# Two cross attention layers on one core: exponentials kept in the score bank, products of n and u1 made earlier, and a row term carried through DRAM

## The reference

```python
# x (32, 256, 512); ctx (32, 256, 256); all float32
q = x @ Wq + bq;  k = ctx @ Wk + bk;  v = ctx @ Wv + bv          # layer 0
w = softmax(q @ k.T / sqrt(512), axis=1)      # over the 256 query rows
y = w @ v + x
n = (y - mean(y)) * rsqrt(var(y) + 1e-6)
x = n * gamma + beta
Q = x @ Wq1 + bq1;  K = ctx @ Wk1 + bk1;  V = ctx @ Wv1 + bv1    # layer 1
a = softmax(Q @ K.T / sqrt(512), axis=-1)
out = x + (a @ V) @ Wo1 + bo1
```

## Time and profile before

| | us |
|---|---|
| median of 3 runs (lowest, highest) | 729.48 (728.43, 730.53) |
| the profiled execution, device time | 729.61 |
| its span, first to last instruction | 727.5 |
| mean granted TensorE clock, share of full speed | 0.993 |

### The profile page before, as it was taken

How to read it: one execution, slowest core, us unless ns; L and a number is a source line. 1 busy time by engine, 2 the same in 40 slices (tenths; PEclk the granted TensorE clock), 3 DMA queues, 4 the chain that set the end, 5 groups by cost and what they waited for, 6 DMA issues and landing times.

```text
span 727.5 us, 12504 instructions
## 1 busy us (share of the span) xinstructions
PE 691.4 (95%) x4107; PEld 598.8 (82%) x4107; DVE 571.3 (79%) x1235; ACT 429.7 (59%) x1040; POOL 495.7 (68%) x391
## 2 busy tenths in 40 slices
PE   8987999999999999999999999999999999999987
PEld 6864888888888888888888888888888888888876
DVE  4899587877968787787878778787877779787764
ACT  2745557466565756656575665757565575656542
POOL 0276958769495876949586794958678494957680
PEclk9999999999999999999999999999999999999999
DMA  8801004040120404012040402104040210401003
GB/s 296 282 1 57 32 1 145 1 145 0 47 97 0 144 0 144 0 61 83 0 144 0 144 0 84 61 0 144 0 144 0 90 55 0 144 0 59 1 0 117
DMA packets 30336, 49.50 MB, mean 68 GB/s; under 512 B 2160, under 2 KB 10352, under 8 KB 30320
## 3 DMA queue, kind: packets, MB, share of 16 engines
q1 hardware_dynamic: 30320, 49.29, 20.0%
HBM read 32.51 MB, written 16.78 MB: 68 GB/s over the span
## 4 chain that ended last, share of the span: by engine, by line
PE 51%; POOL 25%; issue 8%; ACT 8%; DVE 6%; DMA 1%; SPq 0%; POOLq 0%; DVEq 0%; ACTq 0%
PE bank L388 46%; POOL xprod L1177 10%; POOL r L1200 8%; PE bank L395 4%; POOL prod L1168 4%; ACT xT_hi L635 3%; POOL y_lo L1183 2%; ACT prod L721 2%; DVE n L835 1%; PE bank L408 1%; DVE n L1001 1%; ACT cn_even_hi L751 1%; ACT cT_even_hi L635 1%; ACT cn_odd_hi L751 1%; DMA wk_sb<-in_L_xattn_Wk_dram 1%
## 5 line engine op out<-in xcount | busy, mean ns | idle before, releaser
L1160 POOL TENSOR_TENSOR rstd<-var_eps,minus_half 128x2 f32<-128x2 f32 x32 | 22.4, 699 | 115.5 <-DVE var_eps L997 115.5
L633 ACT ACTIVATE y_hi<-bank,terms 128x512 fp32r<-128x512 f32 x64 | 44.1, 689 | 77.5 <-PE bank L388 77.2
L809 DVE SCALAR_TENSOR_TENSOR y_lo<-bank,terms,y_hi 128x512 fp32r<-128x512 f32 x64 | 45.6, 745 | 55.0 <-ACT y_hi L633 55.0
L1168 POOL TENSOR_TENSOR prod<-n,u_b 128x512 f32<-128x512 f32 x64 | 84.2, 1340 | 0.1
L1207 POOL TENSOR_TENSOR r<-r,beta_b 128x512 f32<-128x512 f32 x60 | 76.1, 1288 | 0.0
L1200 POOL TENSOR_TENSOR r<-n,gamma_b 128x512 f32<-128x512 f32 x60 | 75.7, 1307 | 0.0
L388 PE MATMUL bank<-xT_hi,wqk_hi 128*128 128x512 f32 x128 | 52.7, 412 | 14.9 <-DVE xT_lo L811 14.9
L965 DVE SCALAR_TENSOR_TENSOR w_lo<-e,rinv,w_hi 128x256 fp32r<-128x256 f32 x64 | 58.8, 976 | 4.1 <-ACT w_hi L700 4.1
L635 ACT ACTIVATE pc_hi<-bank 128x512 fp32r<-128x512 f32 x32 | 19.1, 598 | 68.4 <-PE bank L388 68.4
L635 ACT ACTIVATE xT_hi<-bank 128x512 fp32r<-128x512 f32 x64 | 33.0, 605 | 37.1 <-PE bank L395 37.1
L974 DVE SCALAR_TENSOR_TENSOR r<-bank,rinv,r 128x512 f32<-128x512 f32 x60 | 44.6, 745 | 12.7 <-PE bank L388 12.7
(11 more groups left out here) (197 smaller groups left out, 2413.5 us busy)
## 6 DMA issues: line engine op xcount, KB each, us to landing
out_dram<-r SPq DMA_DIRECT2D x15, 1024.0 KB, 5.0
x_even<-in_x_dram SPq DMA_DIRECT2D x8, 1024.0 KB, 7.4
ctxn<-in_ctx_dram SPq DMA_DIRECT2D x16, 512.0 KB, 5.5
x_odd<-in_x_dram SPq DMA_DIRECT2D x8, 1024.0 KB, 7.3
wq_sb<-in_L_xattn_Wq_dram SPq DMA_DIRECT2D x4, 256.0 KB, 3.2
wk_sb<-in_L_xattn_Wk_dram SPq DMA_DIRECT2D x2, 512.0 KB, 7.6
wv_sb<-in_L_xattn_Wv_dram SPq DMA_DIRECT2D x2, 512.0 KB, 9.6
wq_sb<-in_L_xattn_Wq_dram SPq DMA_DIRECT2D x1, 1024.0 KB, 11.4
```

Source lines behind the costliest of these rows:

```text
L633: i = act.activation(dst, at((name, k))[:], ACT.Identity, bias=bias)
L809: i = dve.scalar_tensor_tensor(dst, src, bias, high.bitcast(F32), ALU.add, ALU.subtract)
L1160: pool.tensor_tensor(rstd[:, q], var_eps[:, q], minus_half[:, q], ALU.pow).then_inc(rstd_ready, 1)
L1168: pool.tensor_tensor(prod[j % 2][:], N[:, j, :], u_b[1][:], ALU.mult).then_inc(prod_ready, 1)
```

## The change

Three edits.

1. Row term of layer 0: bank `rb`, its four TensorE transposes and ScalarE's copy are gone. SyncE writes `r0s` to a DRAM row of 512 values (`write_r0`, one element per descriptor), waits for it, and loads that row to all 128 partitions of RB (`spread_r0` on SyncE). The load waits also until the bias rows were added (`x_biased`). Both stand behind the context load and ahead of the store of the pair before. VectorE's `maxima0` waits for `rb_loaded`. In iteration 0 one such pair of transfers stands behind the first load of the next x, and a second one, for the next pair, behind the context load.
2. Exponentials: ScalarE reads E0 and writes the exponentials to the score bank (`probs0`), `w_hi` and `w_lo` read them there, and the bank is free only after `w_lo`. `neg0_ready` and the release of the bank come once per half.
3. Products of n and u1: blocks 0 and 1 are made in the same iteration, ahead of the second `rstd`, and both wait for both blocks of n; blocks 2 and 3 come first in the next iteration and wait for both as well. In the iteration before the last (`before_last`) both `rstd` come first. ScalarE sums blocks 0 and 1 at the very end of its iteration, 2 and 3 in the next one between the context's rounding and `y_hi`, that is ahead of `nT_hi`. `add_beta` is done for four blocks together, ahead of `add_bias`. In iteration 0 `next_row_terms0` moves ahead of `prepare1c`.

```diff
-FRONT = {"xT", "cT", "rb", "y", "s0", "rs", "wc", "pr"}
+FRONT = {"xT", "cT", "y", "s0", "rs", "wc", "pr"}
...
+    r0_rows = nc.dram_tensor("r0_rows", (J * P,), F32).ap()
...
+        def probs0(b, mt):
+            return at(("s0", b))[:, mt * T:(mt + 1) * T]
...
+            def write_r0(ready, spread_before):
+                sp.wait_ge(r0s_ready, ready)
+                if spread_before is not None:
+                    sp.wait_ge(rb_loaded, spread_before)
+                with nc.allow_non_contiguous_dma("512 row terms, one element each"):
+                    sp.dma_start(r0_rows.rearrange("(j p) -> p j", p=P), r0s[:]).then_inc(r0_written, 16)
+            def spread_r0(written, biased):
+                sp.wait_ge(r0_written, written)
+                if biased is not None:
+                    sp.wait_ge(x_biased, biased)
+                sp.dma_start(RB[:], r0_rows.partition_broadcast(P)).then_inc(rb_loaded, 16)
...
+                    if not it.back:
+                        write_r0(1, None)
+                        spread_r0(16, None)
                     sp.wait_ge(filled[BANK["cT", KC - 1]], cT_filled)
                     sp.wait_ge(cn_lo, cn_cut)
                     sp.dma_start(ctxn[:], rows_of(ctx_rows, upcoming)).then_inc(ctx_loaded, 16)
+                    write_r0(r0_made, r0_spread)
+                    spread_r0(r0_in_rows, rb_free)
...
-                    spread_r0(it)                      # TensorE
...
                 for b in range(2):                     # ScalarE, softmax0
-                    act.wait_ge(neg0_ready, it.times(2, b + 1))
                     for mt in range(RM):
                         q = b * RM + mt
-                        if mt == RM - 1:
-                            wait_emptied(act, it, "s0", b)
-                        e = act.activation(E0[:, b, mt, :], E0[:, b, mt, :], ACT.Exp, scale=-1.0,
+                        if mt == 0:
+                            act.wait_ge(neg0_ready, it.times(2, b + 1))
+                        e = act.activation(probs0(b, mt), E0[:, b, mt, :], ACT.Exp, scale=-1.0,
...
                 if it.back:                            # ScalarE, iteration
-                    row_terms(it, (0, 1))
+                    row_terms(it, (2, 3), 1)
+                    shifted_row_terms(it)
...
-                if it.front:
-                    copy_bank(it, "rb", 0, RB[:])
-                if it.back:
-                    row_terms(it, (2, 3))
-                    shifted_row_terms(it)
...
-                if it.more:
+                if it.more and it.back:
                     next_row_terms0(it)
+                if it.front:
+                    row_terms(it, (0, 1), 0)
...
                     if b == 0:                         # VectorE, maxima0
-                        wait_emptied(dve, it, "rb")
+                        dve.wait_ge(rb_loaded, it.times(16, 16))
...
-                        dve.scalar_tensor_tensor(W[1][:, b, mt, :], E0[:, b, mt, :], rinv0[:, q:q + 1],
-                                                 W[0][:, b, mt, :].bitcast(F32), ALU.mult, ALU.subtract)\
-                           .then_inc(w_lo, 1)
+                        i = dve.scalar_tensor_tensor(W[1][:, b, mt, :], probs0(b, mt), rinv0[:, q:q + 1],
+                                                     W[0][:, b, mt, :].bitcast(F32), ALU.mult, ALU.subtract)
+                    i.then_inc(emptied[BANK["s0", b]], 1)
...
+            def row_products(it, blocks, back):        # GpSimd
                 for j in blocks:
-                    pool.wait_ge(n_ready, it.times(J, j + 1 - J))
+                    pool.wait_ge(n_ready, it.times(J, max(j, blocks[-1]) + 1 - back * J))
...
                 if it.back:                            # GpSimd, iteration
-                    row_products(it, (0, 1))
+                    row_products(it, (2, 3), 1)
...
                 if it.back:
-                    add_beta(it, (0, 1))
+                    add_beta(it, range(J))
...
                 if it.front:
                     add_bias(it)
-                if it.back:
-                    add_beta(it, (2, 3))
-                if it.front:
-                    rstds(it)
+                    rstd_of(it, 0)
+                    if it.before_last:
+                        rstd_of(it, 1)
+                    if it.j is None and it.known == 0:
+                        wait_emptied(pool, it, "u1")
+                    row_products(it, (0, 1), 0)
+                    if not it.before_last:
+                        rstd_of(it, 1)
```

More of the change, by code:

```diff
@@ L36 @@
 EPS = 1e-6
[L39 removed]
+FRONT = {"xT", "cT", "y", "s0", "rs", "wc", "pr"}
 def tiles(name, n):
     return [(name, k) for k in range(n)]
[L46 removed]
+STEADY = (tiles("xT", 4) + tiles("cT", 2) + tiles("y", 2) + tiles("nT", 4) + tiles("s0", 2)
           + tiles("y1", 2) + [("wc", 0), ("rs", 0), ("wc", 1)] + tiles("s1", 2) + tiles("pr", 2) + tiles("pt", 2)
@@ L61, in place_banks @@
     for t in STEADY:
-        if t[0] in ("rb", "rs"):
-            bank[t] = (turn + (3 if t[0] == "rb" else 4)) % BANKS
+        if t[0] == "rs":
+            bank[t] = (turn + 4) % BANKS
         else:
@@ L258, in two_cross_attentions @@
         hi = {n: sem(f"{n}_hi_ready") for n in ("xT", "cT", "cn", "y", "w", "wc", "nT", "y1", "pt", "pc")}
-        cn_lo, w_lo, w_lo_added = sem("cn_lo_ready"), sem("w_lo_ready"), sem("w_lo_added")
+        cn_lo, w_lo_added = sem("cn_lo_ready"), sem("w_lo_added")
+        r0_written, rb_loaded = sem("r0_rows_written"), sem("rb_loaded")
         r0_ready, r0s_ready, exp0_ready = sem("r0_ready"), sem("r0s_ready"), sem("exp0_ready")
@@ L546, in weigh0 @@
             def weigh0(it, b):
-                pe.wait_ge(w_lo, it.times(2 * RM, (b + 1) * RM))
+                wait_emptied(pe, it, "s0", b)
                 if b == 0:
@@ L715, in bias_of_rows, with row_terms @@
                 act.activation(bias[j], bv0_b[:], ACT.Copy, scale=rs[:, j:j + 1]).then_inc(bias_ready, 1)
-            def row_terms(it, blocks):
+            def row_terms(it, blocks, back):
                 for j in blocks:
-                    act.wait_ge(prod_ready, it.times(J, j + 1 - J))
+                    act.wait_ge(prod_ready, it.times(J, j + 1 - back * J))
                     act.activation(prod[j % 2][:], prod[j % 2][:], ACT.Copy,
@@ L786, in iteration @@
                 if begin_it:
+                    next_row_terms0(it)
                     prepare1c(it)
@@ L940, in maxima0 @@
                                                      neg0[:, q:q + 1])
-                        i.then_inc(*((emptied[BANK["s0", b]], 1) if mt == RM - 1 else (neg0_ready, 1)))
+                    i.then_inc(neg0_ready, 1)
             def maxima1(it):
@@ L1154, in bv_wo, with rstd_of @@
                                        ALU.add).then_inc(bvwo_ready, 1)
[L1156 to L1162, removed]
+            def rstd_of(it, b):
+                pool.wait_ge(var_ready, it.times(2, b + 1))
+                q = slice(b * RT, (b + 1) * RT)
+                pool.tensor_tensor(rstd[:, q], var_eps[:, q], minus_half[:, q], ALU.pow).then_inc(rstd_ready, 1)
+            def row_products(it, blocks, back):
                 for j in blocks:
-                    pool.wait_ge(n_ready, it.times(J, j + 1 - J))
+                    pool.wait_ge(n_ready, it.times(J, max(j, blocks[-1]) + 1 - back * J))
                     if j >= 2:
-                        pool.wait_ge(r1_ready, it.times(J, j - 1 - J))
+                        pool.wait_ge(r1_ready, it.times(J, j - 1 - back * J))
                     pool.tensor_tensor(prod[j % 2][:], N[:, j, :], u_b[1][:], ALU.mult).then_inc(prod_ready, 1)
@@ L1180, in add_w_lo @@
             def add_w_lo(it):
-                pool.wait_ge(w_lo, it.times(2 * RM, 2 * RM))
+                wait_emptied(pool, it, "s0", 1)
                 pool.tensor_tensor(w_lo_sum.rearrange("p (b t) -> p b t", b=2), W[1][:, :, 0, :].bitcast(F32),
```

14 lines of the change are left out of this document (7 added, 7 removed).

## The result

The changed kernel takes 809.68 us (808.3 to 811.7, 4 runs), before 730.0: ratio 1.1096, 95% interval 1.1062 to 1.113. It is 11% slower; 708 was forecast, with 0.05 on the rival that a slow element write makes it slower. The profiled execution took 811.7, its span is 809.9, 82.4 us over the span before.

A forecast was written before the change was run, and what follows sets the result against it. TensorE, at 95%, was taken as the bound. 24.6 us of steady gains less 1.8 for prologue and 1.8 for tail gave 21.0 off 729.61: 708.6, said as 708, range 703 to 717.

The forecast's parts named there:

- The two transfers, steady: Element write, broadcast and store on SyncE in a steady iteration: claimed to cost nothing, with the write's landing free up to 4.0 us.
- D: Landing time of the element write of r0s to DRAM: taken as 3 us, bounds 2.0 and 9.8.
- the rival on the other side: Element write lands after more than 5.7 us, each us over 4.0 coming back 14 times; at 9.8, 790 us; chance 0.05.
- the prologue: Before iteration 1: RB lands at 38 (36.5 to 41), delaying maxima0; iteration 1 comes 1.8 us later (0.5 to 5).
- Wait for xT_lo: TensorE's wait each steady iteration: no product runs beside n, VectorE wins 1.77 us ahead of xT_lo; gain 0.85 us.
- Wait at row_sums: TensorE's wait for y_lo each iteration: w_lo falls from 4.05 to 1.68 us, y_lo comes before TensorE; gain 0.49 us.
- The rb transposes: Ahead of scores0 on TensorE: removing them lets the scores take their place, as y_lo ends just before; gain 0.39 us.
- Steady sum: Gains of the steady iteration together: 1.73 us a period, period 40.35, 24.6 us in all.
- Tail: Last iteration: sums ahead of nT_hi make y1 wait for its lo; costs 1.8 us (0 to 4).
- add_beta ahead of add_bias: Four add_beta behind y_lo on GpSimd delay the first bias: claimed hidden, with 1.4 us to spare.

The follow-up runs named there:

- e2_dram_alone: Kernel before with only the pair of DRAM transfers in place of the rb transposes; 819.54 us, ratio 1.1233.
- e4: Changed kernel with the DRAM row laid out by partition, 128 runs of 16 bytes, and RB read with a step of four; 708.53 us.
- e10: Changed kernel with, from the second write on, 512 single elements 512 bytes apart to another DRAM tensor, RB loaded from the first write's row; 711.59 us.
- e11: Changed kernel with the row written as 256 runs of 8 bytes and RB read with a step of two; 710.88 us.
- e13: e10 with 8 bytes instead of 512 from one single element to the next; 711.47 us.
- e9: Changed kernel writing, from the second write on, only one of four columns of r0s, 128 single 4-byte elements side by side; 809.23 us.
- e12_filler: Changed kernel with 22 useless matmuls put into TensorE's wait ahead of row_sums in iterations 1 to 14; 800.56 us.
- e1_no_dram: Changed kernel with the DRAM transfers undone, rb transposes and ScalarE's copy back; exponentials in the bank and moved products stay; 704.85 us.
- e6_bank_alone: Kernel before with only the exponentials put in the score bank; 717.24 us, ratio 0.9853.
- e5_no_dram_tail: e1_no_dram with ScalarE rounding nT ahead of the sums of products 2 and 3 in the last iteration; 700.73 us.

## Why the prediction was wrong

**The step that failed: "The two transfers, steady".** D was bounded by 2.0 and 9.8 and taken as 3, "nearer to the first", because the queue is empty. It is 8.2 (e2_dram_alone; SyncE's wait in the kernel after is 8.1). An empty queue was no reason for a short landing: behind the same queue the forms of e4 and e10 land after 1.4 and 1.8. The form of the write decides, which no term of the sum had. Of the two rows that I weighed, one was a store in large pieces, the other a load, and neither wrote single neighbouring elements: the value between them was a guess, and 0.05 for everything above 5.7 was far too little. The mechanism is the rival on the other side: a landing over 4.0 comes back in 14 iterations. The point from which it decides fits the runs as far as they go: landings of 3.2 and 3.9 us cost next to nothing (mean periods of 40.36 and 40.34 in e11 and e13), 1.4 wins no more (40.31 in e4), and 7.4 and 8.2 cost some 7 us a period. Nothing between 3.9 and 7.4 was run, and that each us comes back whole isn't shown: from 8.2 to 7.4 (e9) the mean period fell by 0.45, not 0.8.

**Its price was too small.** For 8.2 that rival gives 14 x 4.2 - 21 = 38 us slower, measured are 80. Of the missing 42: the store lands after 7.5 us, not 6.0 (14 x 1.5 = 21). It starts late: in the kernel after nothing moves for 2.7 us behind the broadcast's issue at 457.55, while in e13, with the same transfers in the same order up to the load of x, the first bytes show 0.9 us behind it (issue 477.49) and the store lands after 5.6. The context, issued earlier than in e13, comes only at 460.02 and can't be the cause of that; why the queue starts late behind the dense write stays open. Further, the clock, which I held at 0.993, falls in the waits (9, e12_filler); the prologue costs 6.0 instead of 1.8 (4), as the write holds RB until 42.4, beyond my 41. Some 8 us stay unassigned.

**The page.** "DMA: Bandwidth & Descriptors" of the Trainium skill has about 2 us fixed ("Anatomy of one DMA — SWDGE (gpsimd) path", a fit for transfers issued by GpSimd, which the prediction took over for SyncE's) and a read-modify-write under 512 B ("Specifications"). The trace doesn't agree with the first for this write, 8.2 us, and is not far off it for e4 and e10, 1.4 and 1.8. Being under 512 B isn't what is slow by itself: e10's elements have 4 bytes each. Read-modify-writes of one stretch one behind the other would fit the table above; the runs show the dependence on density, not that mechanism.

**Wait for xT_lo, 0.85:** right in kind, 1.1 in size. The row of the bracket counts from the modelled end of the last transpose. From the start of the x transposes to the first y matmul it is 239.16 - 235.52 = 3.64 us before and 2.54 in e1_no_dram (428.15 to 430.69).

**Wait at row_sums, 0.49:** right in kind, too small for the same reason. From the last matmul ahead of `row_sums` to its matmul with the sum of `w_lo` it is 1.35 us before (256.81 to 258.16) and 0.58 in e1_no_dram (408.13 to 408.71): 0.77. e6_bank_alone, which removes this wait alone, has a period shorter by 0.76. Its cause, `w_lo` at 4.05, was right too; that the moved products would remove half of it without the bank was not seen.

**The rb transposes, 0.39:** wrong, the period fell by 0.06. The step was that TensorE could take up the scores in the transposes' place, as `y_lo` ends 0.07 us before them. But the first score matmul starts 0.46 us after the end of `y_lo` before, 0.47 in e1_no_dram, and 0.45 in e4, without the transposes: `y_lo` set its start all along, and they lay in that lag. The row's order of two ends was no proof of which one TensorE waited for.

**Steady sum:** 1.73 forecast; e1_no_dram's period is 1.81 shorter, e4's 1.87. The errors of these three cancel.

**Tail, 1.8:** 1.7 in the kernel after, but 3.2 in e1_no_dram (632.02 to 702.3, before 660.40 to 727.5), where the wait is 3.0 us and the matmuls behind it are slower; e5_no_dram_tail takes it away. **add_beta ahead of add_bias:** hidden, as said.

## What to carry to other kernels

Small values that go through DRAM should be written as runs of 16 bytes or more, or apart from each other: 512 neighbouring 4-byte writes held the queue for 8 us here, the same 2 KB as 128 runs 1.4, and a reader can take the changed order with a step. With a step of four values VectorE's `maxima0` took 0.61 us a time instead of 0.42 (e4), with a step of two 0.42 (e11). Before such a write is put on a queue, ask what is issued behind it and by when that has to land; here a store that a scaling on GpSimd waited for closed the loop. Even a write that lands fast wants a look at the prologue, where nothing covers it. And where two bounds of an unknown are on both sides of the point that decides, the chance must lie on both sides too.

## What the hardware showed that I had not expected

The landing of the 2 KB write by its form: 8.2 us dense (7.4 with a quarter of the elements), 3.9 and 3.2 at half that density, 1.4 as 128 runs of 16 bytes, 1.8 as 512 elements far apart. The dense write's packets show for about 1 us, and for the rest of its 8 us the DMA engines show nothing. A store that is queued behind it before it has landed begins to move, stands still and goes on when the write ends: 10.5 us for a 1 MB store that took 5.0. And what is issued behind the landing still starts 2.7 us after its issue instead of 0.9 (the kernel after, e13). TensorE, after a wait of 5.6 us, ran some 4 us at half its clock (0.51 granted), with 22 idle matmuls in the wait at full clock.
